# Attention with a learned distance bias: the row stacks of q and k read with the repeated row as inner dimension, and the running maxima stored and loaded by ScalarE instead of GpSimd

## The reference, cut to what matters

```python
B, S, D_MODEL, H = (8, 512, 256, 16)     # batches, rows, width, heads of 16
q, k, v = (heads of layernorm(x) @ Wq.T, @ Wk.T, @ Wv.T)
scores = jnp.einsum('bhqd,bhkd->bhqk', q, k) * SCALING + position_bias   # bias by distance, per head
attn = jax.nn.softmax(scores, axis=-1)
ctx = jnp.einsum('bhqk,bhkd->bhqd', attn, v)
x = x + ctx @ Wo.T
x = x + mixture_of_experts(layernorm(x))  # 7 routed experts, top 2, and a shared one
```

## Time and profile before

| | us |
|---|---|
| median of 3 runs | 1061.87 (1061.54 to 1061.93) |
| the profiled execution's own time | 1057.47 |
| its span | 1055.7 |
| TensorE busy | 969.4 (92% of the span) |
| VectorE busy | 704.8 (67%) |
| ScalarE busy | 514.2 (49%) |
| GpSimd busy | 109.4 (10%) |

### The profile page before, as it was taken

One profiled execution on the slowest core, in us unless ns is written; L12 is line 12 of the kernel. 1 busy time (PEld: TensorE's weight loads), 2 busy tenths in 40 slices (PEclk: granted clock), 3 DMA queues, 4 the chain that ended last, 5 costly groups with the idle time before them and its releaser, 6 DMA issues. The chain is left out here.

```text
span 1055.7 us, 20280 instructions
## 1 busy us (share of the span) xinstructions
PE 969.4 (92%) x7264; PEld 721.2 (68%) x7264; DVE 704.8 (67%) x2048; ACT 514.2 (49%) x680; POOL 109.4 (10%) x245
## 2 busy tenths in 40 slices
PE   5799368999999998999999769999999999999998
PEld 3688145566655665566565449898988888888887
DVE  5565467777767777777786267676766666666764
ACT  3344015666656665666666635444434344444433
POOL 1120011111111111111111000000000000000000
PEclk9899559999999999999999969999999999999999
DMA  5997534323443333333334332010201020201000
GB/s 114 323 321 257 196 93 119 103 94 98 133 129 97 99 125 109 107 99 99 93 93 125 101 105 80 22 59 21 61 21 61 1 79 0 79 1 41 1 21 20
DMA packets 63923, 100.26 MB, mean 95 GB/s; under 512 B 9464, under 2 KB 37648, under 8 KB 63806
## 3 DMA queue, kind: packets, MB, share of 16 engines
q1 hardware_dynamic: 60594, 97.48, 29.3%
q0 software_dynamic: 3072, 1.11, 0.8%
q10 hardware_dynamic: 172, 0.56, 0.2%
HBM read 63.67 MB, written 34.93 MB: 93 GB/s over the span
## 5 line engine op out<-in xcount | busy, mean ns | idle before, releaser
L678 DVE CUSTOM_DVE_ANT_0 sums<-pS,near 128x512 bf16<-128x512 f32 x512 | 325.3, 687 | 125.4 <-PE pS L738 123.7
L709 ACT ACTIVATE prob<-pE 128x1024 f32<-128x1024 f32 x256 | 260.7, 1024 | 209.8 <-PE pE L763 209.3
L1185 PE MATMUL pD<-w2p,h_p 128*128 128x256 f32 x1536 | 203.0, 285 | 1.8 <-DVE x L1035 1.8
L738 PE MATMUL pS<-k_st,q_st 48*128 48x512 f32 x512 | 167.2, 497 | 40.6 <-DMA k_st<-k_parts 27.4
L1185 PEld LDWEIGHTS pD<-w2p,h_p 128*128 128x128 f32 x1536 | 191.4, 188 | 11.2 <-DVE x L1035 2.7
L763 PEld LDWEIGHTS pE<-bandT,place 64*128 64x128 f32 x2048 | 182.5, 190 | 16.1
L1167 PE MATMUL pU<-x2T,w1p 128*128 128x512 f32 x768 | 191.4, 399 | 0.0
L738 PEld LDWEIGHTS pS<-k_st,q_st 48*128 48x128 f32 x512 | 72.3, 193 | 171.5 <-DVE nmax L678 128.1
L1098 ACT ACTIVATE h_f<-pU,b1s 128x512 f32<-128x512 f32 x128 | 88.1, 688 | 191.5 <-PE pU L1167 185.7
L763 PE MATMUL pE<-bandT,place 64*128 64x244 f32 (+2 forms) x2048 | 180.1, 272 | 0.0
L1167 PEld LDWEIGHTS pU<-x2T,w1p 128*128 128x128 f32 x768 | 141.4, 190 | 29.4
(11 more groups left out here) (102 smaller groups left out, 575.1 us busy)
## 6 DMA issues: line engine op xcount, KB each, us to landing
x<-in_x SPq DMA_DIRECT2D x16, 512.0 KB, 4.5
q_parts<-qk SPq DMA_DIRECT2D x16, 512.0 KB, 5.0
k_parts<-qk SPq DMA_DIRECT2D x16, 512.0 KB, 4.7
q_st<-q_parts SPq DMA_DIRECT2D x64, 128.0 KB
k_st<-k_parts SPq DMA_DIRECT2D x64, 128.0 KB
ctx<-ctx_sb SPq DMA_DIRECT2D x32, 256.0 KB, 10.8
near<-bias_by_distance SPq DMA_DIRECT2D x16, 448.0 KB, 14.2
v_rows<-vs SPq DMA_DIRECT2D x8, 512.0 KB, 3.2
```

The source lines that it names most:

```text
L678: dve.tensor_tensor_reduce(sums[:, r % 4], pS[:, BANK[r]], near[:, hg % 2, j, lead:lead + S], -1.0, BIG, ALU.add, ALU.min, nmax[:, j, t:t ...
L709: act.activation(prob[:, par, 2 * step:2 * step + 2], pE[:, 2 * (step % 2):2 * (step % 2) + 2], ACT.Exp).then_inc(exp_done, 1)
L738: pe.matmul(pS[:, BANK[unit]], q_st[rows, r, pair, P * t:P * t + P], k_st[rows, r, pair], start=True, stop=True).then_inc(s_mm, 1)
L1185: ins = pe.matmul(pD[:, t2, u], h_p[:, e % 2, a, m, P * t:P * t + P], w2p[:, e, z, m], start=k == 0 and e < NE - 1, stop=k == 5)
```

## The change

Three things. The source of the doubled rows was read as two whole copies of 16 rows, the number of copies being the outermost dimension; it is now read as 16 rows, each row twice (q) or each row of the high part followed by the same row of the low part (k), with the repetition as an inner dimension. q is then stacked as pairs of equal rows and below them the low part; k as pairs of high and low and below them the high part, which gives the same three products. Sizes and the number of DMAs are as before.

The maxima are stored and loaded by ScalarE's queue: the store for step n + 1 behind the exponential of sub-step 2 of step n, the two loads behind that of sub-step 4; those for step 0 stand ahead of everything. GpSimd has the copies of v alone, in a loop of eight rounds of four.

```diff
-    def stacked(t, b, hg, side, part, copies):
-        lead = ((b * 2 + part) * HG + hg) * (HPG * DH * S) + side * (2 * DH * S)
-        return bass.AP(t.tensor, lead, [[0, copies], [2 * S, DH], [1, 2 * S]])
+    PART = HG * HPG * DH * S
+    def stacked(t, b, hg, side, part, inner):
+        lead = (b * 2 + part) * PART + hg * (HPG * DH * S) + side * (2 * DH * S)
+        return bass.AP(t.tensor, lead, [[2 * S, DH], *inner, [1, 2 * S]])
...
             sp.dma_start(raw(q_st[row:row + 2 * DH, r]).rearrange("p j s -> p (j s)"),
-                         stacked(q_dram, b, hg, side, 0, 2)).then_inc(qk_ld[r], 16)
+                         stacked(q_dram, b, hg, side, 0, [[0, 2]])).then_inc(qk_ld[r], 16)
             sp.dma_start(raw(q_st[row + 2 * DH:row + KQ, r]).rearrange("p j s -> p (j s)"),
-                         stacked(q_dram, b, hg, side, 1, 1)).then_inc(qk_ld[r], 16)
-            sp.dma_start(raw(k_st[row:row + DH, r]).rearrange("p j s -> p (j s)"),
-                         stacked(k_dram, b, hg, side, 1, 1)).then_inc(qk_ld[r], 16)
-            sp.dma_start(raw(k_st[row + DH:row + KQ, r]).rearrange("p j s -> p (j s)"),
-                         stacked(k_dram, b, hg, side, 0, 2)).then_inc(qk_ld[r], 16)
+                         stacked(q_dram, b, hg, side, 1, [])).then_inc(qk_ld[r], 16)
+            sp.dma_start(raw(k_st[row:row + 2 * DH, r]).rearrange("p j s -> p (j s)"),
+                         stacked(k_dram, b, hg, side, 0, [[PART, 2]])).then_inc(qk_ld[r], 16)
+            sp.dma_start(raw(k_st[row + 2 * DH:row + KQ, r]).rearrange("p j s -> p (j s)"),
+                         stacked(k_dram, b, hg, side, 0, [])).then_inc(qk_ld[r], 16)
...
             def _(pool):
-                store_max(0)
-                load_max(0)
-                for m in range(NI):
-                    pool.wait_ge(v_ld[m % RING], 16 * (m // RING + 1))
-                    if m >= 2:
-                        pool.wait_ge(pv_done, PV0 + 4 * m - 4)
-                    pool.tensor_copy(v_aug[:, m % 2, :, :, 0:DH], ...).then_inc(v_ready, 1)
-                    if m < NI - 1:
-                        store_max(m + 1)
-                        load_max(m + 1)
+                with pool.Fori(0, QUADS) as i:
+                    for u in range(4):
+                        m = 4 * i + u
+                        wait_apart(pool, passed, v_ld[u], 16 * (i + 1))
+                        wait_apart(pool, passed, pv_done, PV0 + 4 * m - 4)
+                        pool.tensor_copy(v_aug[:, u % 2, :, :, 0:DH], ...).then_inc(v_ready, 1)
...
             def _(act):
+                (store_max and load_max as they were in pool, with act in its place)
                 def slot(n):
                     par = n % 2
                     for step in range(STEPS):
...
                         act.activation(prob[:, par, 2 * step:2 * step + 2], ..., ACT.Exp).then_inc(exp_done, 1)
+                        if step == 2 and n < NI - 1:
+                            store_max(n + 1)
+                        if step == 4 and n < NI - 1:
+                            load_max(n + 1)
...
+                store_max(0)
+                load_max(0)
                 for n in range(NI):
                     slot(n)
```

More of the change, by code:

```diff
@@ L635, in _ @@
                 wait_apart(pool, passed, ones_set, 2)
[L637 to L648, removed]
-                store_max(0)
-                load_max(0)
-                for m in range(NI):
-                    pool.wait_ge(v_ld[m % RING], 16 * (m // RING + 1))
-                    if m >= 2:
-                        pool.wait_ge(pv_done, PV0 + 4 * m - 4)
-                    pool.tensor_copy(v_aug[:, m % 2, :, :, 0:DH],
-                                     v_raw[:, m % RING].rearrange("p (t h e) -> p t h e", t=TT, h=HPG)).then_inc(v_ready, 1)
-                    if m < NI - 1:
-                        store_max(m + 1)
-                        load_max(m + 1)
+                with pool.Fori(0, QUADS) as i:
[3 more added lines that the diff above has]
+                        wait_apart(pool, passed, pv_done, PV0 + 4 * m - 4)
+                        pool.tensor_copy(v_aug[:, u % 2, :, :, 0:DH],
+                                         v_raw[:, u].rearrange("p (t h e) -> p t h e", t=TT, h=HPG)).then_inc(v_ready, 1)
             @block.vector
@@ L702, in _, with store_max, load_max @@
             def _(act):
+                def store_max(m):
+                    act.wait_ge(max_turned, m + 1)
+                    act.dma_start(max_dram[m].rearrange("a j (t i x) -> i (a j t) x", t=TT, i=4), turned[:, m % 2]
+                                  ).then_inc(max_out, 16)
+                def load_max(m):
+                    act.wait_ge(max_out, 16 * m + 16)
+                    for side in range(2):
+                        row = HALF * side + KQ
+                        act.dma_start(raw(q_st[row:row + KM, m % RING]),
+                                      max_dram[m].rearrange("a (p h) s -> h a p s", h=2)[side]).then_inc(max_ld, 16)
                 def slot(n):
```

## The result

| | before | changed |
|---|---|---|
| median, us | 1061.70 | 1031.72 (1029.12 to 1034.82, 4 runs) |
| ratio to before | | 0.972, 95% interval 0.9685 to 0.9756 |
| the profiled execution's own time | 1057.47 | 1034.82 |
| its span | 1055.7 | 1033.0 |

The time fell by 30.0 us to 1031.7; 1029.3 had been forecast. The profiled execution of the changed kernel is the slowest of its four, and that of the kernel before was 4.2 us faster than its median, so the two spans differ by 22.7 only. The sum looks right. Its parts are not, as the trace shows.

What follows compares the result with a forecast made beforehand. TensorE was taken as the bound in attend, stopped mainly by late q and k stack loads on two DMA engines. Gains 10.9 + 16.5 + 3.2 + 0.5 + 1.5 = 32.6 us took the median 1061.87 to 1029.3; range 1021 to 1047.

Steps and rivals of the forecast that it cites:

- Term 1: TensorE's longest wait for q and k stacks, step 1's loads: gain 10.9 us, bounds 10.4 and 10.9.
- Terms 2 to 4: In attend: twelve other stack waits 16.5 us, half-clock dips behind waits 3.2, long half-clock stretch from 108 to 154 0.5.
- the twelve waits (16.5): TensorE's other waits for q and k stacks in attend: all go, gain 16.5 us, lower bound 12.
- Term 5: Barrier before TensorE's first scores, held by SP's near loads on full queues: gain 1.5 us, bounds 0 and 4.
- Both are hidden ... I take 0: ScalarE's issues and the maxima's landing in a step: hidden with 0.3 and 1.3 us to spare, cost 0.
- The rival: Slower: ScalarE stands for the maxima's store, TensorE waits about 1.4 us in 31 steps, 43 us, total 1072; chance 0.08.
- The 0.3 us to spare: Margin between the sixth exponential's end, 316.9, and TensorE's need at 317.22; more if issues don't wait for the exponential ahead.
- GpSimd's loop, 0: GpSimd's copies of v: register waits add tenths of a us under cover, cost 0.
- an estimate of 5.1 us for 32 small pieces behind 4 KB pieces: Store of the maxima from ScalarE: 32 small pieces on an engine, each behind SP's 4 KB piece, 5.1 us more.
- no granted clock of 0.50 after 150: Sign of being right: TensorE's clock in attend is never granted at 0.50 after 150.
- no wait of TensorE for `prob`: Sign of being right: TensorE doesn't wait for the sixth sub-step's `prob`; ScalarE's store lands in under 4 us.

Runs made afterwards that it cites:

- new stacks alone: The changed kernel with the maxima stored and loaded by GpSimd as in the kernel before; 1021.06 us, 0.9633 of the kernel before.
- the repeat: The changed kernel measured once more, nothing altered; 1027.32 us, 0.9695 of the kernel before.
- the move alone: The changed kernel with the old stacks put back, leaving the maxima through ScalarE and GpSimd's new loop; 1210.71 us, 1.1418 of the kernel before.
- q's copies apart: The kernel before with q's two copies as two DMAs of 16 rows each, k's loads unchanged; 1031.07 us, 0.9745 of the kernel before.

## Why the prediction was right, point by point, and where it was wrong

The timelines split the spans in three: to the first exponents, steps 0 to 30, and the rest.

| us | before | changed | new stacks alone |
|---|---|---|---|
| first exponents at | 146.37 | 134.45 | 132.90 |
| from there to those of step 31 | 436.3 | 427.2 | 413.4 |
| from there to the end | 473.0 | 471.3 | 471.1 |

- **Term 1, the wait of 10.9.** Right. From the first scores to the first exponents it was 33.2 us and is 21.4, a gain of 11.8: the wait and about 1 us that VectorE had stood for near loads. What came next was VectorE's chain, as said.
- **Terms 2 to 4, the other waits and the clock, 20.2 together.** The mechanism is right, and the new stacks alone give 22.9. This is close to the twelve waits (16.5), what the two stretches of half clock cost (1.7 each) and 2.8 us more: four waits of the exponents in the kernel before, put down to "issue", are gone too, and no term had them. In the changed kernel 9.1 of the 22.9 is left.
- **Term 5, the barrier, 1.5.** Nothing in the changed kernel's own profile (first scores at 113.18 before and 113.09 after). Over all profiles there is something: the three kernels with the old stacks begin the scores at 113.2 to 113.4, the nine with q's or all copies spread at 110.9 to 113.1, in the median 112.2. That is 1.0 to 1.1 us, near the term.
- **"Both are hidden ... I take 0"**, for the maxima through ScalarE. This is the step that failed. It cost 13.2 us in the first profiled execution and 7.0 in the second; by the medians 10.7, and 6.3 with the repeat. The working took the landing of another store, 2.0 us, and this one takes little more when no bias load is beside it (2.0 to 3.8 with them held back). But 12 steps have bias loads, in six of them the near load is issued within half a microsecond of the store (in eight in the repeat), and it has 448 KB, 28 for each engine; this traffic was in the code and not in the sum. The rival had the place, the wait in ScalarE's order, and a price of 0.9 to 1.9 us above a landing of some 4.2; it was left with 31 steps or none. It came in 6, at 1.0 to 3.4 us, the three dearest with a stretch of half clock behind them; loads 4.76 us behind the store still cost only 0.1.
- **ScalarE's issues.** The 0.3 us to spare was more: an issue doesn't wait for the exponential ahead of it (see the last section), as the working had left open.
- **GpSimd's loop, 0.** Right. "Tenths of a us" was high: the register instruction of a copy takes 46 to 57 ns and its two waiting instructions 17 ns each.
- **The rule of the Trainium skill on two queues that meet on an engine** ("DMA: Bandwidth & Descriptors", Queues, rings and completion order): the engine takes turns between them by packets. From it the prediction worked out an estimate of 5.1 us for 32 small pieces behind 4 KB pieces. In the move alone the loads go out 7.9 to 9.5 us behind the store, 5.7 to 7.3 more than the 2.2 of the store with the bias loads held back. The trace agrees in size, a little above the estimate. That the pieces alternate one by one isn't shown by any run here.
- **The rule of the Trainium skill on the outermost count** ("DMA: Bandwidth & Descriptors", Rules for kernel authors): c copies outermost keep a DMA to at most c engines. The trace agrees: the quiet share of 0.12 with two copies outermost, of 0.04 and 0.05 with 16 rows outermost, and the halved wait with q's copies apart follow it.

So the forecast of 1029.3 came out within 2.4 us by luck in part, with two errors that offset each other: the gain of the stacks was 39.3 us by the medians where 32.6 was forecast, and the cost of the move, taken at 0, was 6 to 11. About 1.9 of the 38.3 us between the profiles of before and of the new stacks alone lie in the last part, which the change doesn't touch; that part takes 471.0 to 473.3 us over the twelve profiles, so differences of 2 us between kernels say nothing about attend. With the wait taken from ScalarE, or the bias loads held back, the same stacks run in 1020.3 to 1021.1, below the kernel before and the changed one; these versions can't be told apart.

Of what was to be seen: no wait for `k_parts`, the earlier first exponents and the quiet DMA engines came; the steps of 13.5 came in all but six; "no granted clock of 0.50 after 150" and "no wait of TensorE for `prob`" were wrong, and the loads of the maxima went out under 4 us behind the store in all steps from 4 to 27 without bias loads, but in only four of the twelve with them.

## What to carry to other kernels

When a load is late, look at the DMA share in a moment when only it can be running: 0.12 of 16 engines is two engines, and the outermost count of the access pattern is the place to look. Before a wait for a DMA is put into the order of an engine that feeds the bound, price the transfer with everything issued within its flight, and give the wait an engine with nothing behind it; here that choice was worth 6 to 11 us. With the old stacks, store and wait on ScalarE together cost 150 us, and the wait alone came with some 5 us (0.7%), with GpSimd's store in time for it; the store alone on ScalarE was not tried with the old stacks.

## What the runs showed of the hardware that was not expected

- The same 16 KB store, old stacks: 5.5 us to landing from GpSimd's software queue, and 7.9 to 9.5 us until the waiting loads went out from ScalarE's hardware queue. In packets the page shows ScalarE's queue with 4780 where it had 172 before; GpSimd's queue had 3072 for the same stores and loads. The trace's packets say what became of the store: 32 stores are 128 packets of 4096 bytes from GpSimd (in the run in which it only stores) and 4096 packets of 128 bytes from ScalarE. How much of the lateness is this and how much the later moment stays open; GpSimd's store at the later moment took up to 5.2 us to land.
- An issue on ScalarE's queue doesn't wait for the exponential ahead of it: the one starts at 263.01 and takes 1.03 us, the other at 263.02. The 0.56 to 0.67 us that each issue takes lie beside the engine's work, and cost nothing that shows.
- TensorE's waits of 1.41, 1.51 and 1.95 us in three of the six long steps were each followed by 3.4 us at 1.2 GHz under full work, those of 0.70, 0.80 and 0.96 in the others were not. The length of the wait doesn't decide it alone: in the kernel before, waits of 1.43 to 1.68 us in steps 1, 18, 19 and 20 were followed by no such stretch.
